# Third norm taken into the elastic attention, tile by tile, with both attentions and both feed-forwards in one block

## The reference, cut to what matters

```python
h = concat([tok(x), txt], axis=1)
h = h + attn0(layernorm(h))                      # first norm
x = layernorm(h)                                 # second norm; its output is the stream of the "elastic" block
nl, ns = ln(x[:8], n1l), ln(x[8:], n1s)
x1 = x + concat([branch(nl), sum(g[i] * branch_i(ns))])      # elastic attention, 12 heads of 16
nl2, ns2 = ln(x1[:8], n2l), ln(x1[8:], n2s)      # THIRD NORM, over the 192 channels of a token
x2 = x1 + concat([mlp(nl2), sum(g[i] * mlp_i(ns2))])         # elastic feed-forward, exact gelu
h = h + x2
h = h + experts(layernorm(h))                    # fourth norm, four experts with windowed attention
h = h + ffn(layernorm(h))                        # last norm and feed-forward
```

## Time and profile before

| | |
|---|---|
| median of three runs | 1216.74 us (1216.56 to 1217.07) |
| the profiled execution's own time | 1217.27 us |
| its span in the profile | 1215.5 us |
| PE busy | 1125.7 us, 93% |
| ACT, DVE, POOL busy | 760.2, 732.4, 479.5 us |
| chain that ended last | PE 60% of the span, every other engine at most 1% |
| elastic attention, first to last instruction | about 213 to 407.4 us |
| third norm, to the first instruction of the feed-forward | 408.3 to 448.3 us |
| elastic feed-forward | 448.3 to 564 us |

### The profile page before, as it was taken

The page is one execution under the profiler, slowest core; times in us unless marked ns, Lnnn a source line. Parts: engine busy times, 40 slices in busy tenths (PEclk is TensorE's granted clock), DMA queues, the critical chain, the costliest instruction groups (busy, mean ns, idle before and its releaser), DMA issues.

```text
span 1215.5 us, 33842 instructions
## 1 busy us (share of the span) xinstructions
PE 1125.7 (93%) x13103; PEld 922.1 (76%) x13103; DVE 732.4 (60%) x2291; ACT 760.2 (63%) x3351; POOL 479.5 (39%) x677
## 2 busy tenths in 40 slices
PE   5689997799999859998999999999999999999898
PEld 4569973677877525644899999999989989998677
DVE  7434447567666520435777777777777777777301
ACT  1145544577677352453888888787878888887411
POOL 2100004333433127453665554545555545565300
PEclk8869995899999759999999999999999999999999
DMA  7100000000000440001000000000000000000000
GB/s 252 27 2 1 2 1 1 1 1 2 2 2 1 88 115 1 1 1 46 3 2 3 3 2 3 2 2 3 2 3 2 2 3 2 3 2 3 1 30 30
DMA packets 34734, 19.84 MB, mean 16 GB/s; under 512 B 24592, under 2 KB 32016, under 8 KB 34576
## 3 DMA queue, kind: packets, MB, share of 16 engines
q1 hardware_dynamic: 34432, 17.20, 5.2%
q10 hardware_dynamic: 144, 0.49, 0.1%
HBM read 15.12 MB, written 1.77 MB: 14 GB/s over the span
## 4 chain that ended last, share of the span: by engine, by line
PE 60%; DVE 1%; ACT 0%; issue 0%; POOL 0%; ACTq 0%; DVEq 0%; POOLq 0%
PE banks L1564 8%; PE banks L1616 7%; PE banks L1576 7%; PE banks L1362 5%; PE banks L1632 5%; PE banks L1604 4%; PE banks L1651 4%; PE banks L2015 3%; PE banks L1972 3%; PE banks L1609 3%; PE banks L1656 2%; PE banks L1592 2%; PE banks L1639 2%; PE banks L1412 1%; PE banks L1215 1%; PE banks L1428 1%
## 5 line engine op out<-in xcount | busy, mean ns | idle before, releaser
L1939 POOL TENSOR_TENSOR e_W<-e_W,e_RS 128x384 f32<-128x384 f32 x256 | 205.1, 827 | 262.1 <-DVE e_RS L1820 261.0
L1756 ACT ACTIVATE e_W<-banks,e_MX 128x128 f32<-128x128 f32 x768 | 268.9, 389 | 15.8 <-DVE e_MX L1808 14.4
L1756 ACT ACTIVATION_READ_ACCUMULATOR e_W<-banks,e_MX 128x1 f32 x768 | 176.3, 230 | 0.0
L1750 ACT COPY e_PT<-banks 128x512 f32<-128x512 f32 x128 | 70.0, 588 | 74.1 <-PE banks L1616 73.8
L1616 PE MATMUL banks<-ident,e_W 128*128 128x128 f32 x768 | 107.6, 274 | 2.9 <-POOL e_W L1939 1.4
L1564 PE MATMUL banks<-XT,e_wqk 128*128 128x141 f32 x768 | 106.2, 288 | 2.0 <-ACT e_K L1745 1.8
L1117 POOL TENSOR_TENSOR f_W<-f_W,f_RS 128x423 f32<-128x423 f32 x64 | 56.4, 892 | 116.6 <-DVE f_RST L1101 108.6
L1564 PEld LDWEIGHTS banks<-XT,e_wqk 128*128 128x128 f32 x768 | 96.0, 190 | 4.3 <-issue 2.5
L1576 PE MATMUL banks<-e_wv,XT 128*128 128x192 f32 (+1 forms) x512 | 95.1, 329 | 0.8 <-ACT e_K L1745 0.8
L1616 PEld LDWEIGHTS banks<-ident,e_W 128*128 128x128 f32 x768 | 86.7, 143 | 6.6 <-DVE e_ON L1845 2.9
L1808 DVE TENSOR_REDUCE e_MX<-banks 128x3 f32<-128x384 f32 x128 | 65.4, 552 | 40.1 <-PE banks L1604 40.1
(11 more groups left out here) (302 smaller groups left out, 2729.9 us busy)
## 6 DMA issues: line engine op xcount, KB each, us to landing
xp<-in_patches_dram SPq DMA_DIRECT2D x4, 768.0 KB, 8.8
H<-in_h_dram SPq DMA_DIRECT2D x1, 1728.0 KB, 11.0
out_dram<-H SPq DMA_DIRECT2D x6, 288.0 KB, 2.3
m_hid<-in_e_gu_dram SPq DMA_DIRECT2D x1, 1536.0 KB, 8.4
m_hid<-in_e_o_dram SPq DMA_DIRECT2D x4, 192.0 KB, 5.7
e_wqk<-in_e_qk_dram SPq DMA_DIRECT2D x8, 96.0 KB, 2.5
e_wqk<-in_e_qk_dram SPq DMA_DIRECT2D x24, 32.0 KB, 2.4
e_wv<-in_e_v_dram SPq DMA_DIRECT2D x4, 192.0 KB, 2.7
```

What stands on the lines that cost most here:

```text
L1750: nc.scalar.copy(PT[:, 4 * u:4 * u + 4, :], bank[4 + u][:, 0:4 * P]).then_inc(s_pa, 1)
L1756: ex = nc.scalar.activation(W[n % 2][:, t, :], bank[i][:, x * P:(x + 1) * P], ACT.Exp, bias=MX[:, t:t + 1], accum_out=SM[n % 2][:, t:t + 1])
L1939: nc.gpsimd.tensor_tensor(x, x, RS[n % 2][:, 3 * i:3 * i + 3].unsqueeze(2).broadcast_to([P, 3, P]), ALU.mult).then_inc(s_nm, 1)
```

## The change

In the elastic attention, iteration n now also does a part of the third norm. With s = n-2, the tiles range(9s//8, 9(s+1)//8) are complete once sample s is finished: one tile for each s, two for s = 7.

- Iteration n from 2 to 16, **back**: PE turns these tiles of `AT` back after `attend(n-1)` (`back_third`), waiting for `finish(n-2)`; DVE adds them to `XN` at the very end of its iteration (`add_third`), and in iteration n+1 forms their statistics after `finish` (`third_stats`). The transposes that open PE's iteration n+1 wait for the addition, as both use bank 4.
- Iteration n+2, so n from 4 to 17, **forward**: POOL norms the tiles at the start of its iteration (`third_norm`), PE turns them into bank 6 between `out_project` and `attend` (`forward_third`), and ACT writes them to `XT` with gain and bias (`evacuate_third`), after the tail's weights and before exponential groups 2 and 3. `project_qk(n+2)`, which writes bank 6 again, waits for ACT.
- What is left goes into the feed-forward: tiles 16 and 17 are turned back between the halves of `up(0)`, tiles 15, 16 and 17 forward between the halves of `up(1)`; ACT takes these three out before the gelus of group 1, and `wide_down(0)` waits for that.
- The separate norm stage is gone, with two meetings of all engines. `load_late` is issued by SP at the start of the elastic attention. Several buffers of the two attentions are now the same ones (`QE`, `KM`, `BQ`, `VP` and the small ones), the weights and masks move to other addresses, and `XN` normed tiles have three buffers (`f_xn`).

The diff, cut to the norm's new steps and their places (the loops of the attention are otherwise as before):

```diff
+            back3_at = {s + 2: range(9 * s // 8, 9 * (s + 1) // 8) for s in range(B - 1)}
+            forward3_at = {s + 4: back3_at[s + 2] for s in range(B - 2)}
+            IN_F, BACK_F = forward3_at[B + 1][-1] + 1, back3_at[B][-1] + 1
+
+            def third_stats(dve, tiles):
+                for i in tiles:
+                    dve.wait_ge(s_r3, i + 1)
+                    nc.vector.bn_stats(stats[:, i, :], XN[:, i, :]).then_inc(s_b3, 1)
+                for i in tiles:
+                    dve.wait_ge(s_b3, i + 1)
+                    nc.vector.bn_aggr(mv[:, i, :], stats[:, i, :]).then_inc(s_m3, 1)
+
+            def third_norm(pool, tiles):
+                lo, hi = tiles[0], tiles[-1] + 1
+                r = slice(lo, hi)
+                pool.wait_ge(s_m3, hi)
+                nc.gpsimd.tensor_scalar(veps[:, r], mv[:, r, 1], 1e-5, None, ALU.add).then_inc(s_v3, hi - lo)
+                pool.wait_ge(s_v3, hi)
+                nc.gpsimd.tensor_tensor(rstd[:, r], veps[:, r], nhalf[:, r], ALU.pow).then_inc(s_p3, hi - lo)
+                pool.wait_ge(s_p3, hi)
+                for i in tiles:
+                    if i >= 3:
+                        pool.wait_ge(s_f3, i - 2)
+                    nc.gpsimd.tensor_scalar(xn3[i % 3][:, :], XN[:, i, :], mv[:, i, 0:1], rstd[:, i:i + 1], ALU.subtract,
+                                            ALU.mult).then_inc(s_x3, 1)
+
+            def back_third(pe, dst, i):
+                pe.wait_ge(sf_fin, (P * i + P - 1) // SLOT * 2 + 2)
+                nc.tensor.transpose(dst[:, 0:P], AT[:, 0, i * P:(i + 1) * P], ident[:, :])
+                nc.tensor.transpose(dst[:, P:C], AT[0:C1, 1, i * P:(i + 1) * P], ident[0:C1, 0:C1]).then_inc(s_t3, 1)
+
+            def forward_third(pe, dst, i):
+                pe.wait_ge(s_x3, i + 1)
+                nc.tensor.transpose(dst[:, 0:P], xn3[i % 3][:, 0:P], ident[:, :])
+                nc.tensor.transpose(dst[0:C1, P:2 * P], xn3[i % 3][:, P:C], ident[:, :]).then_inc(s_f3, 1)
+
+            def evacuate_third(act, src, i, last):
+                act.wait_ge(s_f3, last + 1)
+                v = V_N2L if i < HALF else V_N2S
+                nc.scalar.activation(XT[:, 0, i * P:(i + 1) * P], src[:, 0:P], ACT.Identity, scale=vecs[:, v:v + 1],
+                                     bias=vecs[:, v + 2:v + 3])
+                for lo in (0, C1):
+                    ev = nc.scalar.activation(XT[lo:lo + C1, 1, i * P:(i + 1) * P], src[0:C1, P:2 * P], ACT.Identity,
+                                              scale=vecs[0:C1, v + 1:v + 2], bias=vecs[0:C1, v + 3:v + 4])
+                ev.then_inc(s_e3, 1)
+
+            def add_third(dve, src, i, last):
+                dve.wait_ge(s_t3, last + 1)
+                nc.vector.tensor_tensor(XN[:, i, :], src[:, 0:C], XN[:, i, :], ALU.add).then_inc(s_r3, 1)
+
             WIDE, MG = 3, 6
             m_first = [HM * (g + 2 * max(0, g - WIDE)) for g in range(MG + 1)]
...
+            REST3 = range(BACK_F, TILES)
+            REST3_AT = (bank[6][:, 0:2 * P], bank[6][:, 2 * P:4 * P], bank[7][:, 0:2 * P])
+
             with nc.Block() as block:
+                @block.sync
+                def _(sp):
+                    load_late(sp)
+
...
+                    for n in range(B + 2):
+                        if 1 <= n <= B:
+                            if n - 1 in back3_at:
+                                pe.wait_ge(s_r3, back3_at[n - 1][-1] + 1)
+                            pe.wait_ge(sf_nm, 5 * n - 3)
...
+                            if n >= 3:
+                                pe.wait_ge(sf_fin, 2 * (n - 2))
+                            out_project(n - 2)
+                        if n in forward3_at:
+                            pe.wait_ge(sf_v, 2 * min(n, B - 1) + 2)
+                            for k, i in enumerate(forward3_at[n]):
+                                forward_third(pe, bank[6][:, 2 * k * P:2 * (k + 1) * P], i)
+                        if 1 <= n <= B:
+                            attend(n - 1)
+                        if n in back3_at:
+                            for k, i in enumerate(back3_at[n]):
+                                back_third(pe, bank[4][:, k * C:(k + 1) * C], i)
+                        if n in forward3_at:
+                            pe.wait_ge(s_e3, forward3_at[n][-1] + 1)
+                        if n + 2 < B:
+                            project_qk(n + 2)
...
+                            exponentials(n, 0)
+                            exponentials_tail(n)
+                            exponentials(n, 1)
+                        if 1 <= n <= B:
+                            evacuate_weights(n - 1, 4)
+                            evacuate_tail(n - 1)
+                        if n in forward3_at:
+                            for k, i in enumerate(forward3_at[n]):
+                                evacuate_third(act, bank[6][:, 2 * k * P:2 * (k + 1) * P], i, forward3_at[n][-1])
...
+                        if n < B:
+                            reciprocals(n, 6, 9, 4)
+                        if n >= 2:
+                            finish(n - 2)
+                        if n - 1 in back3_at:
+                            third_stats(dve, back3_at[n - 1])
+                        if n < B:
+                            reciprocals(n, 9, 12, 5)
+                        if 1 <= n <= B:
+                            evacuate_attended(n - 1)
+                        if n in back3_at:
+                            for k, i in enumerate(back3_at[n]):
+                                add_third(dve, bank[4][:, k * C:(k + 1) * C], i, back3_at[n][-1])
+
...
+                    nc.gpsimd.tensor_tensor(m_ii[:, :], ident[:, 0:C1], ident[:, C1:P], ALU.add).then_inc(s_ii, 1)
+                    for n in range(B + 3):
+                        if n - 2 in back3_at:
+                            third_norm(pool, back3_at[n - 2])
+                        if n >= B:
...
@@ -1365,10 +1427,21 @@
 
                     def up_all(g):
 
+                        pe.wait_ge(s_e3, min(3 * g + 3, IN_F))
                         for m in range(HM):
                             if m_first[g] + m >= 6:
                                 pe.wait_ge(s_mgl, m_first[g] + m - 5)
+                            elif m == 4:
+                                pe.wait_ge(s_r3, BACK_F)
+                                pe.wait_ge(sf_o, 2 * B)
                             up_part(g, m, m, 0, 0, P, True, False)
+                        if g == 0:
+                            for k, i in enumerate(REST3):
+                                back_third(pe, bank[6][:, k * C:(k + 1) * C], i)
+                        if g == 1:
+                            pe.wait_ge(s_c, 2 * EXPERTS)
+                            for k, i in enumerate(range(IN_F, TILES)):
+                                forward_third(pe, REST3_AT[k], i)
                         for m in range(HM):
                             up_part(g, m, m, 1, m % 2 * C1, C1, False, True).then_inc(s_mup, 1)
 
...
                                 pe.wait_ge(s_mfn, t - 1)
                             else:
-                                pe.wait_ge(s_c, 2 * EXPERTS)
+                                pe.wait_ge(s_e3, TILES)
...
+                    pe.wait_ge(sf_ex, 5 * B)
                     up(0)
+                    pe.wait_ge(s_r3, TILES)
                     fold_products(pe)
                     for g in range(MG):
...
+                            for k, i in enumerate(range(IN_F, TILES)):
+                                evacuate_third(act, REST3_AT[k], i, TILES - 1)
...
+                    for k, i in enumerate(REST3):
+                        add_third(dve, bank[6][:, k * C:(k + 1) * C], i, TILES - 1)
+                    third_stats(dve, REST3)
...
                     for t in range(TILES):
+                        if t == 2 * GT_ // P:
+                            third_norm(pool, REST3)
```

631 lines of the change are left out of this document (296 added, 335 removed).

## The result

The changed kernel takes **1243.94 us** (median of 4 runs, 1241.08 to 1247.11) against 1216.76 us before (four runs, 1216.56 to 1217.07): ratio **1.0224, 95% interval 1.0197 to 1.0250**. It is 2.2% slower. The prediction said 1214.9 with a range of 1209 to 1222, so it is wrong by 29 us. The profiled execution of the change has a span of 1241.2 us at a mean granted clock of 0.941, the one before 1215.5 at 0.951. A single run further down, one of ten of before_finish, was slow (1323.24 us at a granted clock of 0.818) and is left out.

What follows compares the result with a forecast made beforehand. PE was taken to bound the attention and no engine the norm. Norm stage -39.4, attention +35.8, feed-forward +3.6, warm up(0) -1.75 sum to -1.8 us: from 1216.74 to 1214.9 us, range 1209 to 1222.

Steps and rivals of the forecast that it cites:

- What goes, -39.4 us: Separate norm stage and its two meetings of all engines between attention and feed-forward: removing them saves 39.4 us.
- Twelve iterations, 31.6 us: Attention iterations 4 to 15, with back and forward work: each grows by 2.63 us, together 31.6 us.
- the rival of the shorter chain: Attention iterations: faster activations or overlapping hand-overs, each growing only 2.2 to 2.4 us; 1210 to 1212 us; 21%.
- Iterations 9 and 11: Attention iterations with two tiles: 9 turns two back, 0.46 us more; 11 turns two forward, 1.5 us more.
- The feed-forward, 3.6 - 1.75 us: Leftover tiles in up(0), up(1) and the wait of wide_down(0) add 3.6 us; a warm up(0) saves 1.75 us.
- The loads: Feed-forward loads now beside the attention: zero cost; as a rival, 4 us from disturbed iterations, 1219 us, 9%.
- a rival at 16%: New PE holes in the attention let the clock fall, 1.75 us per fall; slower from the third fall; 16%.
- Falls in all twelve iterations: Extreme of the clock falling in the attention: a fall in every one of the twelve iterations gives 1236 us.
- the prediction's own sign of being wrong: Attention: the prediction is wrong if the clock drops there, or the period is under 13.5 or over 14.5 us.
- dense `attend` before it: Before each new PE hole stands attend, dense but on quarter-width tiles; weighed in the clock's chance, without its own size.
- the chain: Attention iteration: forward pair, XT writes, exponential group 2, finish, back pair in sequence; PE waits 1.9 us, iteration grows 2.63 us.

Runs made afterwards that it cites:

- before_finish: Kernel before the change, with finish and third_stats on DVE moved ahead of the reciprocal of exponential group 2; 1218.70 us, ratio 1.0005.
- fill12: Changed kernel plus 12 unread filler transposes on TensorE in the hole between attend and the back pair, iterations 4 to 15; 1220.96 us, ratio 1.0021.
- fill3: Changed kernel plus 3 unread filler transposes on TensorE in the hole between attend and the back pair; 1229.45 us, ratio 1.0079.
- fill6: Changed kernel plus 6 unread filler transposes on TensorE in the hole between attend and the back pair; 1228.52 us, ratio 1.0073.
- act_order: Changed kernel with exponential group 2 moved ahead of the three XT writes on ACT, DVE order unchanged; 1203.96 us, ratio 0.9860.
- dve_order: Changed kernel with DVE reordered: finish, third_stats, evacuate_attended, reciprocal of group 2, add_third, reciprocal of group 3; 1201.95 us, ratio 0.9863.
- before_hole: Kernel before the change, plus 5 unread ACT copies per sample and a TensorE wait for finish before project_qk, samples 4 to 15; 1230.50 us, ratio 1.0102.
- before_hole9: before_hole with 9 copies on ACT instead of 5; 1250.29 us, ratio 1.0240.
- before_hole10: before_hole with 10 copies on ACT instead of 5; 1248.04 us, ratio 1.0246.

## Why the prediction was wrong

**What goes, -39.4 us: right.** At the new seam PE waits for ACT's three `XT` writes 1.80 us; I had 1.6.

**Twelve iterations, 31.6 us: right.** 13.99 us where I had 14.01; the hole 1.71 where I had 1.9. The three activations take 0.43 us each, as the row said (290.59 to 291.88), so the rival of the shorter chain, at 23%, was nothing. (The sum starts tile 14's forward pair at 406.97, 0.08 us before its own 407.05, for which no row stands.) Iterations 9 and 11 cost 0.46 and 1.51 us more than their neighbours (14.46 and 15.51 in fill12; 0.46 and 1.5 predicted).

**The feed-forward, 3.6 - 1.75 us: right in the change, by luck in part.** `wide_down(0)` waits 1.90 us as predicted, and the first projections run warm (4.11 us for the first twelve). But fill3, fill6, act_order and dve_order have the same wait before them, and there the clock falls within 1.1 us behind it (5.80 us for the same twelve in fill6). Nor did the sum price a fall behind the wait of 1.90.

**The loads: right.** Zero within the spread.

**The step that failed is the clock.** The sum took a granted clock of 1.00 through the twelve new holes, so it put the falls at nothing, and kept them as a rival at 16%. Measured, they cost 22.5 us before the feed-forward's first matmul, and the prediction's own sign of being wrong, a clock that drops in the attention, is what came. With the clock held in the attention (fill12) the kernel is 0.21% above the one before (0.01 to 0.41), where the sum had 0.15% below, and its profile still holds falls at 474, 576 and 1143 us. Without that help, the clock fell eight times in or up to 1.7 us behind the change's holes, and once before them. Two things were mis-sized in the rival. A fall was priced at 1.75 us, what a cold projection loses; here a short one costs 15.62 - 13.99 = 1.63 us, but a long one 17.04 - 13.99 = 3.05, since the lower level lasts 6.8 us and covers the projection, the transposes and part of the scores behind it (the long ones with less of dense work under them cost less, down to 16.29 - 13.99 = 2.30 in the steady part, and the one at 238 us, behind a wait of 0.72 us that the kernel before has there too, 253.20 - 249.64 = 3.56 against fill12). Falls in all twelve iterations were to give 1236; eight gave more. And the chance was far too low. The earlier trace rows showed two holes and gave the second as one that fills 1140 to 1141 us; in the timeline of before it is 2.08 us long, longer than the new ones, and two more that passed stood there as well:

```profile
567.93 1.68 PE L1564 MATMUL banks<-XT,e_wqk 128*128 128x141 f32 x12 [1.82 <-ACT e_K L1745]
...
575.73 0.30 PE L1676 MATMUL banks<-ident,XN 128*128 128x128 f32 x1 [2.04 <-ACT e_W L1756]
...
1141.66 0.33 PE L1991 MATMUL banks<-ident,AT 128*128 128x128 f32 x1 [2.08 <-POOL AT L1922]
```

So of four holes of 1.8 to 2.1 us that began at full clock, one was followed by a fall. An estimate from that, twelve times one in four, gives three falls, which by the prediction's own price is 1220: it should have been in the forecast and not in a rival. I let "dense `attend` before it" decide, with no row behind it. What the Trainium skill describes (TensorE: Matmul & The Clock Gate, section A second HAM failure mode: psum-queue depth-cycling), and the prediction set against its own number, is what the trace of the change shows: with short pauses of TensorE between groups of matmuls in every iteration the clock swings between its levels, 47.6 us of 220 at the lower one. Pauses of 0.76 us in every iteration of before_hole did not do it from 290 to 410 us.

A second error is one of method. The sum listed what the chain costs and did not ask whether the chain had to be. The timeline of before shows DVE idle ahead of that reciprocal already, with `finish` behind it:

```profile
340.55 0.18 DVE L1052 RECIPROCAL f_RS<-f_SM 128x3 f32<-128x3 f32 x1 [1.75 <-ACT f_W L989]
```

An order that cuts the chain turns the same change from 2.2% slower into 1.4% faster.

**Shown:** the falls cost about 22 us (fill12); they follow from the holes (fill12, dve_order and act_order take the holes and all but one fall away, before_hole9 brings both without the norm); the chain makes the holes (dve_order, act_order). **Open:** why the falls in the changed kernel last 6.8 us and recur sample after sample, while those in the kernel before with a hole as long are rarer and last 3.4. before_hole10 differs in the period (13.20 against 13.99) and in the two thin pairs around the hole; neither was tried alone. The falls at 599 and 1145 us, behind the changed part, begin 1.5 and 1.0 us after holes that the kernel before has too (2.04 us at 575.73, 0.94 at 1120.59) and passed without a fall; in before_finish it fell behind both. Which of these holes brings a fall in a given kernel stays open.

```profile
598.21 0.30 PE L1755 MATMUL banks<-ident,XN 128*128 128x128 f32 x1 [2.04 <-ACT e_W L1835]
...
1144.83 0.63 PE L1695 MATMUL banks<-ident,e_W 128*128 128x128 f32 x4 [0.94 <-POOL e_W L2018]
```

## What to carry to other kernels

When a step is threaded through a loop that TensorE bounds, look for the wait that it makes at TensorE and price it twice: its length, and the granted clock that may fall in it; here the second was worth as much as the first (22 us beside 12 x 1.71 = 20.5). Before accepting such a wait, read what stands ahead of the awaited instruction in its own engine's list; a better order of DVE's calls was worth 40 us. Count the holes of that length that the trace already has, with and without a fall behind them, before a chance is put on it. If the hole can't be removed, matmuls that nobody reads are a cheap test of how much of a loss is the clock.
